# Pairwise attention and recurrent layers on one core: which queue brings the values back, and when the first pairs are loaded

## The reference, cut to what matters

```python
lk = (x @ W_lk).reshape(b, n, n, H, DK)   # b = 2, n = 64, H = 8, DK = 32
rk = (x @ W_rk).reshape(b, n, n, H, DK)
lv = (x @ W_lv).reshape(b, n, n, H, DK)
rv = (x @ W_rv).reshape(b, n, n, H, DK)
scores = jnp.einsum('bxahd,bayhd->bxayh', lk, rk) / np.sqrt(DK)
att = jax.nn.softmax(scores, axis=2)
o = jnp.einsum('bxayh,bxahd,bayhd->bxyhd', att, lv, rv)
```

## Time and profile before

| | us |
|---|---|
| median of 3 runs | 4064.18 (4056.3 to 4067.26) |
| the profiled execution's own time | 4066.59 |
| its span | 4064.8 |
| first stage, to about 304 | 304 |
| mixing, about 304 to 1139 | 835 |
| all that follows | 2926 |

### The profile page before, as it was taken

The page is one execution under the profiler, slowest core; times in us unless marked ns, Lnnn a source line. Parts: engine busy times, 40 slices in busy tenths (PEclk is TensorE's granted clock), DMA queues, the critical chain, the costliest instruction groups (busy, mean ns, idle before and its releaser), DMA issues. The chain is left out here.

```text
span 4064.8 us, 80462 instructions
## 1 busy us (share of the span) xinstructions
PE 3614.2 (89%) x29903; PEld 2939.1 (72%) x29903; DVE 2862.5 (70%) x4169; ACT 2412.4 (59%) x6208; POOL 1261.3 (31%) x708
## 2 busy tenths in 40 slices
PE   8977888788879979999999989999999687788887
PEld 5644555455558868888888878888888544688886
DVE  1558999899947754777777746777777544677787
ACT  3546888788845545666666645666566310577776
POOL 0008999899935532000000020000000000122254
PEclk9989999999989989999999989999999899999999
DMA  4573111311123332000000030000000143544565
GB/s 126 167 218 81 42 43 44 80 42 42 40 71 105 107 100 83 17 17 17 16 17 11 12 97 17 17 17 16 17 25 13 41 139 137 161 137 136 146 209 166
DMA packets 204739, 303.61 MB, mean 75 GB/s; under 512 B 18464, under 2 KB 156576, under 8 KB 201376
## 3 DMA queue, kind: packets, MB, share of 16 engines
q1 hardware_dynamic: 195232, 291.51, 23.8%
q10 hardware_dynamic: 9216, 8.39, 0.6%
HBM read 199.18 MB, written 100.66 MB: 74 GB/s over the span
## 5 line engine op out<-in xcount | busy, mean ns | idle before, releaser
L661 POOL TENSOR_TENSOR mx_big<-mp_lvs,mx_big 128x1280 f32<-128x1280 f32 (+1 forms) x256 | 801.6, 3212 | 330.0 <-ACT mp_lvs L587 313.2
L640 DVE TENSOR_TENSOR mx_big<-mp_psL,mx_big 128x2816 f32<-128x2816 f32 (+1 forms) x256 | 785.8, 3146 | 38.4 <-PE mp_psO L532 31.4
L594 ACT ACTIVATE mp_cut<-mp_psO,mx_mask 128x128 f32<-128x128 f32 x2048 | 550.8, 404 | 143.5 <-PE mp_psO L532 113.1
L1228 PE MATMUL sv_psO<-at_v_hi,sv_p_hi 128*128 128x258 f32 x2048 | 584.2, 285 | 13.1 <-DVE sv_p_lo L1316 10.1
L532 PE MATMUL mp_psO<-mx_big,mp_pair 128*16 128x256 f32 x8192 | 500.1, 384 | 107.2 <-DVE mx_big L640 88.8
L1228 PE MATMUL sv_psO<-at_v_lo,sv_p_hi 128*128 128x258 f32 x2048 | 578.8, 283 | 0.0
L1228 PE MATMUL sv_psO<-at_v_hi,sv_p_lo 128*128 128x258 f32 x2048 | 578.5, 282 | 0.0
L1247 ACT COPY sv_S<-sv_psS 128x512 f32<-128x512 f32 x512 | 300.5, 587 | 379.1 <-PE sv_psS L1202 282.9
L532 PEld LDWEIGHTS mp_psO<-mx_big,mp_pair 128*16 128x16 f32 x8192 | 326.3, 126 | 244.4 <-DVE mx_big L640 135.8
L1291 DVE TENSOR_TENSOR sv_run<-sv_run,sv_S 128x512 f32<-128x512 f32 x448 | 316.6, 707 | 248.4 <-ACT sv_S L1247 247.6
L1316 DVE TENSOR_TENSOR sv_p_lo<-sv_S,sv_p_hi 128x512 fp32r<-128x512 f32 x512 | 353.9, 691 | 107.5 <-ACT sv_p_hi L1256 106.8
(11 more groups left out here) (218 smaller groups left out, 6979.9 us busy)
## 6 DMA issues: line engine op xcount, KB each, us to landing
re_xg<-xg SPq DMA_DIRECT2D x192, 384.0 KB, 3.3
xg<-ga_xg SPq DMA_DIRECT2D x32, 768.0 KB, 3.7
att<-mx_big SPq DMA_DIRECT2D x16, 1024.0 KB, 5.5
mx_big<-rv SPq DMA_DIRECT2D x16, 1024.0 KB, 17.7
mp_pair<-att SPq DMA_DIRECT2D x128, 128.0 KB, 2.9
fr_xr<-in_x SPq DMA_DIRECT2D x16, 512.0 KB, 4.9
fr_xl<-in_x SPq DMA_DIRECT2D x32, 256.0 KB, 4.2
rv<-fr_rvs SPq DMA_DIRECT2D x16, 512.0 KB, 2.9
```

Of the source, the lines that this page charges most:

```text
L594: ins = nc.scalar.activation(cut[:, s, c, :, h * DK:(h + 1) * DK], psO[:, c % 2, :, h * DK:(h + 1) * DK], ACT.Copy, scale=mask[:, h:h + 1])
L640: nc.vector.tensor_tensor(Z[:, c % 2, 0:m], psL[:, s, 0:D].unsqueeze(1).broadcast_to([P, m, D]), big[:, rv_slot(b, c), 0:m], ALU.mult).the ...
L661: nc.gpsimd.tensor_tensor(Z[:, c % 2, m:YC], lvs[:, s, :].unsqueeze(1).broadcast_to([P, YC - m, D]), big[:, rv_slot(b, c), m:YC], ALU.mult ...
L1228: mm = pe.matmul(psO[:, j, 0:VW], a[:, u % 2, j * P:(j + 1) * P], x[:, c, :], start=(i == 0 and e == 0), stop=(i == SC - 1 and e == len(te ...
```

## The change

1. The 8 DMAs that read the first batch's values back are issued by ACT, after its copies of block 13, and no longer by SP.
2. After the 16 blocks SP loads xin and pair of the first two steps, before the stores of the second batch. xin, pair and their semaphores belong to both stages; pair's zeros are written by POOL in the first stage. The second stage no longer waits for the zeros.
3. The stage's end waits for the first four stores of the second batch (chunks 4 to 7) alone; the other four have a semaphore of their own, waited for before slots 4 and 5 are loaded.
4. In the second stage SP loads steps 2 and 3, then values c = 0 and 1 of batch 1, then the rest. Values c = 2 and 3 are issued by ACT, in step 31, behind its cuts 0 and 1.
5. To make room, some small tiles of the first stage share memory (run2 and sum2; den for both batches; rdenT lies in xlT).

```diff
 # attention_weights, SP
-                    if j == max(SUMS):
-                        sp.wait_ge(att_out[0], 16 * NC)
-                        sp.wait_ge(dve_summed, NHALF - 1)
-                        for t in range(2):
-                            sp.wait_ge(rv_out[t], 16 * (NC // 2))
-                        for c in range(N // YC):
-                            load_rv(sp, big, rv_d, 0, c, rv_back)
+                for s in range(2):
+                    load_pair_x(sp, shared["xin"], x, 0, s, s, done["x_in"][s])
+                sp.wait_ge(att_out[0], 16 * NC)
+                for s in range(2):
+                    load_pair_weights(sp, shared["pair"], att, 0, s, s, done["a_in"][s])
                 for k in range(NC):
                     save(1, k)
...
-                sp.wait_ge(att_out[1], 16 * NC)
+                sp.wait_ge(att_out[1], 16 * (NC // 2))
...
 # attention_weights, ACT, at the end of block j
+                    if j == max(SUMS):
+                        load_values()     # the same waits, then load_rv(act, ...) x4
...
 # attention_weights, POOL
+                nc.gpsimd.memset(pair[0:N, :, 1], 0.0).then_inc(pair_cleared, 1)
+                nc.gpsimd.memset(pair[N:P, :, 0], 0.0).then_inc(pair_cleared, 1)
...
 # mix_pairs, SP
-                sp.wait_ge(zeroed, 2)
...
                 for s in range(2):
-                    load(0, s, s)
+                    load(0, 2 + s, s)
+                sp.wait_ge(att_out[2], 16 * (N // 16))
                 for c in (0, 1):
                     load_rv(sp, big, rv_d, 1, c, rv_in[c])
-                with sp.Fori(1, NH // 2) as i:
+                with sp.Fori(2, NH // 2) as i:
                     for s in range(2):
                         load(0, i * 2 + s, s)
-                load(1, 0, 0)
-                for c in (2, 3):
-                    sp.wait_ge(z_dve, HEAD + (NH - 1) * NQ + c - 1)
-                    sp.wait_ge(z_pool, HEAD + (NH - 1) * NQ + c - 1)
-                    load_rv(sp, big, rv_d, 1, c, rv_in[c])
-                load(1, 1, 1)
-                with sp.Fori(1, NH // 2) as i:
+                with sp.Fori(0, NH // 2) as i:
...
 # mix_pairs, ACT
                     cut_heads(n, s, 0)
+                    if n == NH - 1:
+                        load_values(2)
                     if n + 1 < NXP:
                         keep_xT(n + 1, 1 - s)
                     cut_heads(n, s, 1)
+                    if n == NH - 1:
+                        load_values(3)
...
 # mix_pairs, DVE
-                nc.vector.memset(pair[0:N, :, 1], 0.0).then_inc(zeroed, 1)
-                nc.vector.memset(pair[N:P, :, 0], 0.0).then_inc(zeroed, 1)
```

More of the change, by code:

```diff
@@ L88, in mix_phase @@
         shared = {"ident": ph.sb("ident", [P, P]), "wlv": ph.sb("wlv", [P, KT, D]), "big": ph.sb("big", [P, 2 * N // YC, YC, D]),
-                  "sel": ph.sb("sel", [P, 4, 32]), "mask": ph.sb("mask", [P, H]), "norm": ph.sb("norm", [P, B, G, HG, N // 2])}
-        attention_weights(nc, shared, x, FRONT["w_lk"], FRONT["w_rk"], w_lv, w_rv, ident_d, sel_d, mask_d, att, rv_d)
-        mix_pairs(nc, shared, x, att, rv_d, o_d)
+                  "sel": ph.sb("sel", [P, 4, 32]), "mask": ph.sb("mask", [P, H]), "norm": ph.sb("norm", [P, B, G, HG, N // 2]),
+                  "xin": ph.sb("xin", [P, 2, D]), "pair": ph.sb("pair", [P, 2, 2, H, N])}
+        done = {"x_in": [ph.sem(f"x_in{s}") for s in range(2)], "a_in": [ph.sem(f"a_in{s}") for s in range(2)],
+                "att_out": [ph.sem("att0_out"), ph.sem("att1_out_67"), ph.sem("att1_out_45")]}
+        attention_weights(nc, shared, x, FRONT["w_lk"], FRONT["w_rk"], w_lv, w_rv, ident_d, sel_d, mask_d, att, rv_d, done)
+        mix_pairs(nc, shared, x, att, rv_d, o_d, done)
 YC = 16
@@ L111, in by_partition, with load_pair_x, load_pair_weights, attention_weights @@
     return att.rearrange("b x a f -> (b x a f)").rearrange("(b p a f) -> b p a f", b=B, p=P, a=N)
-def attention_weights(nc, shared, x, w_lk, w_rk, w_lv, w_rv, ident_d, sel_d, mask_d, att, rv_d):
+def load_pair_x(eng, xin, x, b, i, s, done):
+    eng.dma_start(xin[:, s, :], x[b, bass.ds(i * 2, 2)].rearrange("x a d -> (x a) d")).then_inc(done, 16)
+def load_pair_weights(eng, pair, att, b, i, s, done):
+    rows = by_partition(att)[b].rearrange("(g x) a f -> x a g f", g=G)
+    for c in range(2):
+        eng.dma_start(pair[c * N:(c + 1) * N, s, c].rearrange("a (g h) y -> a g (h y)", g=G),
+                      rows[bass.ds(i * 2 + c, 1)].rearrange("o a g f -> (o a) g f")).then_inc(done, 16)
+def attention_weights(nc, shared, x, w_lk, w_rk, w_lv, w_rv, ident_d, sel_d, mask_d, att, rv_d, done):
     ident = shared["ident"]
@@ L160, in attention_weights @@
         rv_out = [fr.sem(f"rv_out{s}") for s in range(2)]
-        att_out = [fr.sem(f"att_out{s}") for s in range(B)]
+        att_out = done["att_out"]
         rv_back = fr.sem("rv_back")
+        pair_cleared = fr.sem("pair_cleared")
         xr_turned, xl_turned, xrT_kept, xlT_kept = (fr.sem(n) for n in "xr_turned xl_turned xrT_kept xlT_kept".split())
@@ L327, in keep_norms, with load_values @@
                     nc.scalar.copy(shared["norm"][:, b].rearrange("p g h n -> p (g h n)"), psT[:, 1, 0:N * G * HG // 2]).then_inc(norm_kept, 1)
+                def load_values():
+                    act.wait_ge(att_out[0], 16 * NC)
+                    act.wait_ge(dve_summed, NHALF - 1)
+                    for t in range(2):
+                        act.wait_ge(rv_out[t], 16 * (NC // 2))
+                    for c in range(N // YC):
+                        load_rv(act, big, rv_d, 0, c, rv_back)
                 for j in range(NJ):
@@ L396, in invert @@
                     dve.wait_ge(dve_summed, sums[0])
-                    fold(sum2[:, :, :], sum4[:, 0:2, :], sum4[:, 2:4, :])
-                    fold(den[:, b, 0, :], sum2[:, 0, :], sum2[:, 1, :])
-                    last = den[:, b, 0, :]
+                    fold(two[:, :, :], sum4[:, 0:2, :], sum4[:, 2:4, :])
+                    fold(den[:, 0, :], two[:, 0, :], two[:, 1, :])
+                    last = den[:, 0, :]
                     if PE_SUMS[b]:
@@ L433, in _, with mix_pairs @@
                 invert(1)
-def mix_pairs(nc, shared, x, att, rv_d, o_d):
+            @block.gpsimd
+            def _(pool):
+                pair = shared["pair"]
+                nc.gpsimd.memset(pair[0:N, :, 1], 0.0).then_inc(pair_cleared, 1)
+                nc.gpsimd.memset(pair[N:P, :, 0], 0.0).then_inc(pair_cleared, 1)
+                pool.wait_ge(pair_cleared, 2)
+def mix_pairs(nc, shared, x, att, rv_d, o_d, done):
     NH = N // 2
     NXP = B * NH
-    ident, wlv, big, sel, mask, norm = (shared[n] for n in "ident wlv big sel mask norm".split())
+    ident, wlv, big, sel, mask, norm, xin, pair = (shared[n] for n in "ident wlv big sel mask norm xin pair".split())
     with ExitStack() as stack:
@@ L457, in mix_pairs @@
         rv_in = [mp.sem(f"rv_in{c}") for c in range(NQ)]
-        x_in = [mp.sem(f"x_in{s}") for s in range(2)]
-        a_in = [mp.sem(f"a_in{s}") for s in range(2)]
-        zeroed = mp.sem("zeroed")
+        x_in, a_in, att_out = done["x_in"], done["a_in"], done["att_out"]
         psO_clear = mp.sem("psO_clear")
@@ L482, in load @@
                     sp.wait_ge(turned, HEAD + n - 1)
[L483 removed]
+                    load_pair_x(sp, xin, x, b, i, s, x_in[s])
                     sp.wait_ge(z_used, HEAD + (n - 1) * NQ)
[L485 to L488, removed]
+                    load_pair_weights(sp, pair, att, b, i, s, a_in[s])
                 for s in range(2):
[L491 removed]
+                    load(0, 2 + s, s)
+                sp.wait_ge(att_out[2], 16 * (N // 16))
                 for c in (0, 1):
                     load_rv(sp, big, rv_d, 1, c, rv_in[c])
[L494 removed]
+                with sp.Fori(2, NH // 2) as i:
                     for s in range(2):
                         load(0, i * 2 + s, s)
[L497 to L503 removed]
+                with sp.Fori(0, NH // 2) as i:
                     for s in range(2):
```

24 lines of the change are left out of this document (12 added, 12 removed).

## The result

The changed kernel took 4070.7 us (median of 14 runs, 4061.25 to 4289.1) and the kernel before 4062.74 us (median of 14, 4055.7 to 4069.48) in the same comparison: +8.0 us. The ratio is 1.0018 with a 95% interval of 1.0010 to 1.0027, so it is slower, by less than 0.3%. By the ratio that is +7.3 us (4.1 to 11.0). The forecast was +8.5 us.

The account below looks back on a forecast made before the run. PE was taken to pace the first stage, DVE and POOL products the mixing. Terms +4.8 (values on ACT), +5.9 (mixing start) and -2.2 (change of batch) gave +8.5 on 4064.2: 4072.7 us, range 4060 to 4081.

Parts of the forecast that it names:

- The stage's end, 0: End of the first stage: letting half of the last stores run on frees nothing, as ACT's copy ends later; 0 us.
- The values on ACT's queue, +4.8: First stage after block 13: ACT issues 8 DMAs before copying the transposes, so PE's next turn comes later; +4.8 us.
- PE's next turn slides by the same 4.8: First stage: PE's turn at 223.22, right behind ACT's copy into the single PSUM transpose tile, comes 4.8 us later.
- The stall unchanged: Score(14) in the first stage: PE's 7.91 us wait for an instruction transfer keeps its length.
- Rival A: Score(14): the instruction block comes at its old time, so the stall takes in ACT's delay; sum +3.7, 4067.9 us; chance 0.22.
- B: As a rival: in score(14) the instruction block comes still later, stall up to 7.9 us longer; sum +16.4, 4080.6 us; chance 0.14.
- The assumption behind the term: Score(14): the instruction transfer is asked for as PE uses up the block before it, so it moves with PE.
- Start of the mixing, -4.5 - 2.1 + 12.5: Mixing start: PE turns 4.5 us sooner, step 1's xin wait goes (-2.1), step 4's xin waits behind values (+12.5); +5.9 us.
- Change of batch, -2.2: Step 32: the wait for xin goes, but ACT issues the values later, so their landing still holds the products; -2.2 us.
- ACT issues c = 2 after cut 0 of step 31: Change of batch: ACT's first issue of these values comes at 714.0 instead of 709.7.
- Rival C: Change of batch comes free: c = 3 lands by 730, term -9.8; sum +0.9, 4065.1 us; chance 0.12.

Follow-up runs that it names:

- e1: The changed kernel run again with no edit; ratio 1.0010 to the kernel before (4067.3 against 4064.8 us by the medians).
- e10: The changed kernel with the first stage's end waiting for all eight stores of the second batch, as before the change; 4070.6 us, one run.
- e2: The changed kernel with the first batch's values issued by SP after block 13's rv store, as before; ratio 1.0005 to the kernel before.
- e7: e5 with the first values read back after block 15's rv store instead of block 13's; ratio 0.9966 to the kernel before.
- e9: e5 with the first values issued by SP only once score(14) is done; 4047.4 us against 4064.0 for the kernel before, ratio 0.9948.
- e3: The changed kernel with batch 2's values 0 and 1 issued by ACT, one 1 MB DMA in each of steps 3 to 6; ratio 0.9993 to the kernel before.
- e4: The changed kernel with values 2 and 3 issued by SP between the loads of steps 32 and 33, as before; ratio 1.0025 to the kernel before.
- e11: e9 with the first stage's end waiting for all eight stores of the second batch; 4056.7 us, ratio 0.9978 to the kernel before.
- e5: The changed kernel with the edits of e2 and e3 together; ratio 0.9958 to the kernel before.

## Why the prediction was right, and where it was off

The time (+8.0, forecast +8.5) and the sign of each term came out. That the two numbers are so close is luck: two terms were off and partly cancelled, the stretches add up to +5.7, and e1's own comparison gave +2.5 by the medians.

- **The stage's end, 0.** Right, and shown by e10: B does not move.
- **The values on ACT's queue, +4.8.** Right in mechanism, too small: +6.1 between the profiles, 5.2 between e1 and e2. The step "PE's next turn slides by the same 4.8" gave 4.0 us of standing (ACT began to issue 0.16 us into its last copy, not after it: 217.04 against 216.88), and I left out that PE comes back from the pause at a granted clock of 0.63, which made 3.60 us of matmuls 5.29.
- **The stall unchanged.** Right in size: 8.13, and 7.4 to 8.7 in all nine kernels, the one before among them, that loaded the values at block 13. That these loads make all of it but 2.2 us is shown by e7, where they come later. Rival A is out, and B as well: it stayed although ACT's queue carried the values and SP's a live store. The assumption behind the term held too: in the four profiles with ACT's issues the instruction transfer began 26.3 to 27.3 us after block 13's last copy, in the five with SP's 20.3 to 21.6. The Trainium skill (Runtime: NRT & Kernel Launch, Instruction fetch mechanics) gives PE a store of 128 KiB and calls the cost of going from one 16 KiB block to the next mostly hidden. Score(14) of e9, without a wait, agrees; the nine stalls of 7.4 to 8.7 us, and the 5.3 to 5.6 us in score(11) of all twelve profiles, do not.
- **Start of the mixing, -4.5 - 2.1 + 12.5.** Right: -4.5, and +9.8 for the rest, where 10.4 was forecast; the wait for xin was 10.63 us against 10.6. e3 shows the cause by taking it away (12.2 us in the stretch).
- **Change of batch, -2.2.** It was -5.7 (4.1 against e4, whose PE had more clock after the wait). The step that failed is "ACT issues c = 2 after cut 0 of step 31", read as after that cut has ended. In e1 the first issue came 5.4 us after step 31's first product (718.68 against 713.31), and by the forecast it would have been 8.3 (714.0 against 705.7). It came 0.1 us after PE had ended mix 0 of step 31 (718.56), which is what cut 0 waits for, and before the activations of cut 0 began (719.39). ACT gives a DMA out while its earlier activations still run, as it also did at 217.04 in stretch A. That is 2.9 us of the 3.5 that were missing; the values took 22.4 us and not 23.3, another 0.9. The two make 3.8; D scatters by 0.5 us among the profiles with ACT's issues (69.0 to 69.5). Rival C (change free, -9.8) did not come: DVE waits 5.74 us for the DMA.
- The sum of the stretches is 5.7, the first comparison says 8.0 (4.1 to 11.0 by the ratio's interval), and that of e1 4.1 (-0.4 to 8.5); one profile against another cannot say more than that.

What stays open: why the stall is the same for pieces of 256 KB and of 1 MB, and which property of the loads delays the instruction transfer. Also why e7 still stalls for 2.16 us in score(14) and e9 does not, with the values not yet under way in either, and what PE waits for in score(11), which no run changed. There two stores of exponents and a load of x had just been issued, and the DMA engines were 85% busy (188 to 193.7 us before).

## What to carry to other kernels

Before a DMA issue is moved to another engine, read what that engine does next and who waits for it: eight issues of 0.63 us were free on SP and cost 5 to 6 us on ACT, because PE stood behind ACT's next copy. A large load should not go ahead of a small one that is due in the same queue: 4 MB in a row cost 12 us in the stretch, the same 4 MB as one DMA a step cost none. And a relaxed wait is worth nothing until it is the last one to end: the half of the stores left under way gave 0 here and 10 us once the values had been moved behind score(14).

## What the runs showed of the hardware that I had not expected

- PE's waits with "issue" as cause grow when bulk loads are under way: 7.4 to 8.7 us in score(14) with the values loading, whether from SP's or ACT's queue and in pieces of 256 KB or 1 MB; 2.16 us without them (e7), none when they start just after (e9 and e11). In score(11) it is 5.3 to 5.6 us in all twelve profiles, with stores of 1 MB and a load of x under way. In the nine long stalls of score(14) PE went on 2.8 to 3.0 us after one transfer of 16 KB on the instruction queue q8 had begun.
- A pause of PE of 4 us (e1) was followed by a granted clock of 0.63 in the next 3.8 us: the lower of the two levels (1.2 GHz, a share of 0.5) for most of that stretch. Behind the stall of 8.73 us in e5 it was 0.51 over 3.8 us, and 1.00 in the 4 us after. So a stall costs more than its length: block 15 took 24.5 us in e5, with a stall of 8.73, and 13.7 in e9 without one.
- An engine can stand in a DMA issue when its queue holds large loads: four small DMAs took SP 27.60 us in e9 behind 8 MB of values on its own queue, and 2.55 us in e1. That a full queue is the reason is my reading; no view shows how full a queue is.
